# Perceiver block: token tiles normalised on POOL and gathered one by one, slot weights inside the scan loop, another order of POOL's drives

## What is computed

```python
x = x + cross_attention(ctx_1024, layernorm(x))      # 16 heads, keys and values from 1024 + 64 rows
x = x + mamba(layernorm(x))                          # see below
x = x + experts(layernorm(x))                        # see below

# mamba: xz = norm(x) @ W_in; conv of 4 taps, silu; dt = softplus(..); 16 states n per channel:
h[n] = exp(dt * A[n]) * h[n] + dt * B[n] * x         # a scan over the 64 tokens of a sequence
y    = sum_n h[n] * C[n] + x * D
out  = (y * silu(z)) @ W_out + residual

# experts: 8 experts, each with a list of 512 tokens (top_idx), W1 256x1024, W2 1024x256
gathered = x[top_idx.T]
out_e = gelu(gathered @ W1 + b1) @ W2 + b2
out[token] += out_e * combine_weight[token, e]
```

## Time and profile before

| | |
|---|---|
| time, median of 3 runs | 818.61 us (818.13 to 819.67) |
| the profiled execution | 817.9 us, of which the span from first to last instruction is 816.2 |
| busy in the span | PE 742.0 us (91%), DVE 513.0, POOL 417.0, ACT 415.3 |
| mean granted TensorE clock | 0.964 of 2.4 GHz |
| chain that ended last, by engine | PE 55%, POOL 15%, DVE 14%, issue 9%, ACT 4%, DMA 2% |
| attention and its fillers | up to about 650 us |
| last tile of the mamba layer | about 650 to 721.6 us |
| norm and gather | 721.6 to 738.1 us |
| experts and output | 738.1 to 816.2 us |

### The profile page before, as it was taken

The page is one execution under the profiler, slowest core; times in us unless marked ns, Lnnn a source line. Parts: engine busy times, 40 slices in busy tenths (PEclk is TensorE's granted clock), DMA queues, the critical chain, the costliest instruction groups (busy, mean ns, idle before and its releaser), DMA issues.

```text
span 816.2 us, 14312 instructions
## 1 busy us (share of the span) xinstructions
PE 742.0 (91%) x5387; PEld 677.1 (83%) x5387; DVE 513.0 (63%) x1104; ACT 415.3 (51%) x1118; POOL 417.0 (51%) x375
## 2 busy tenths in 40 slices
PE   4979999999999999999999999999998675889996
PEld 2569999999988999998889899888988562468885
DVE  5355556557564776888777769885798686840102
ACT  2534544554355566655566555466666264604331
POOL 3817105402620299668647986775588899500000
PEclk9999999999999999999999999999999966979998
DMA  8550020010002100300210121100111119203710
GB/s 312 216 154 2 1 65 15 1 65 15 1 1 65 41 14 14 95 14 11 67 46 9 13 72 46 12 11 1 30 20 27 23 21 343 105 0 104 259 51 29
DMA packets 48696, 48.81 MB, mean 60 GB/s; under 512 B 18340, under 2 KB 43632, under 8 KB 47472
## 3 DMA queue, kind: packets, MB, share of 16 engines
q1 hardware_dynamic: 48624, 47.85, 19.4%
HBM read 43.45 MB, written 4.26 MB: 58 GB/s over the span
## 4 chain that ended last, share of the span: by engine, by line
PE 55%; POOL 15%; DVE 14%; issue 9%; ACT 4%; DMA 2%; SPq 0%; POOLq 0%; DVEq 0%; ACTq 0%
PE psum L1587 15%; PE psum L1620 12%; PE psum L1603 4%; PE psum L1976 3%; POOL work L608 3%; PE psum L1966 3%; POOL y_sum L621 3%; POOL work L615 3%; PE psum L1560 2%; DVE work L918 2%; PE psum L1540 2%; PE psum L1642 2%; DMA wq_sb<-in_L_xattn_Wq_dram 2%; DVE rowmax L981 1%; PE psum L1670 1%
## 5 line engine op out<-in xcount | busy, mean ns | idle before, releaser
L1266 ACT ACTIVATE pt_hi<-psum 128x512 fp32r<-128x512 f32 (+1 forms) x192 | 87.3, 489 | 208.4 <-PE psum L1603 155.7
L1620 PE MATMUL psum<-kvn_hi,pt_hi 128*128 128x256 f32 x512 | 150.1, 293 | 1.0 <-DVE pt_hi L838 1.0
L1620 PE MATMUL psum<-kvn_hi,pt_lo 128*128 128x256 f32 x512 | 144.3, 282 | 0.0
L1620 PE MATMUL psum<-kvn_lo,pt_hi 128*128 128x256 f32 x512 | 144.3, 282 | 0.0
L981 DVE TENSOR_REDUCE rowmax<-psum 128x1 f32<-128x728 f32 x64 | 58.6, 915 | 82.1 <-PE psum L1587 81.9
L1620 PEld LDWEIGHTS psum<-kvn_hi,pt_hi 128*128 128x128 f32 x512 | 97.5, 190 | 1.3 <-DVE pt_hi L838 1.2
L1620 PEld LDWEIGHTS psum<-kvn_lo,pt_hi 128*128 128x128 f32 x512 | 97.7, 191 | 0.1
L1620 PEld LDWEIGHTS psum<-kvn_hi,pt_lo 128*128 128x128 f32 x512 | 97.3, 190 | 0.0
L1587 PE MATMUL psum<-kvt_hi,qk_hi 128*128 128x364 f32 (+1 forms) x384 | 90.8, 345 | 6.8 <-ACT prob L1386 4.3
L615 POOL TENSOR_TENSOR work<-work,bc 128x512 f32<-128x512 f32 x48 | 65.8, 1372 | 53.6 <-DVE work L918 53.6
L841 DVE TENSOR_TENSOR pt_lo<-psum,pt_hi 128x512 fp32r<-128x512 f32 x128 | 82.0, 682 | 8.7 <-ACT pt_hi L1266 8.7
(11 more groups left out here) (235 smaller groups left out, 1568.2 us busy)
## 6 DMA issues: line engine op xcount, KB each, us to landing
w<-in_L_ffn_W_dram SPq DMA_DIRECT2D x16, 1024.0 KB, 8.4
ctx_nat<-in_ctx_dram SPq DMA_DIRECT2D x8, 1024.0 KB, 5.2
bc<-dbc_keep SPq DMA_DIRECT2D x48, 128.0 KB, 4.7
q_keep<-q_t SPq DMA_DIRECT2D x1, 2048.0 KB, 8.4
q_cur<-q_keep SPq DMA_DIRECT2D x14, 128.0 KB, 3.1
wk_nat<-in_L_xattn_Wkv_dram SPq DMA_DIRECT2D x1, 1024.0 KB, 6.2
wq_sb<-in_L_xattn_Wq_dram SPq DMA_DIRECT2D x1, 1024.0 KB, 12.7
wv<-in_L_xattn_Wkv_dram SPq DMA_DIRECT2D x1, 1024.0 KB, 14.8
```

The costliest lines, as they stand in the source:

```text
L1266: act.activation(pt_hi[u][:, t0:t1, :], where[:, 0:(t1 - t0) * P].rearrange("p (t m) -> p t m", m=P), ACT.Copy)\
L1620: pe.matmul(PV, w[u][:, j, :], x_[slot][:, j, :], start=(j == 0 and w is pt_hi and x_ is kvn_hi), stop=False)
```

## The change

1. **POOL's order for pair 3.** Before: drives 0, 1, open, drive 2, close, drive 3, close, drive 4, close, gate, drives 5 to 15. After: drives 0, 1, open, drives 2, 3, then three times a closing followed by two drives (4 to 9), the gate, drives 10 to 15. The wait for `ld_ball` now stands ahead of the first of these closings.
2. **`w_out` of pair 2 and its addition.** PE does it after sum 13 (before: 8), DVE adds it behind scan 15 (before: 11).
3. **Slot weights.** PE computes those of two experts (eight matmuls) after each of the sums 11 to 14.
4. **Norm.** DVE takes the statistics of tiles 0 and 1 ahead of the loop, of tile 2 behind read 15, of tile 3 behind its addition. POOL, behind its last drive, does variance and power of each tile by itself, and for tiles 0 to 2 `f_nat` and `f_lo` too, with ACT's `f_hi` between them. Tile 3 stays on DVE. `f_nat` of the four tiles now lies in the two `dec` buffers.
5. **Gather.** PE adds tile by tile: group 1 of tile 0 before `w_out` of pair 3, group 1 of tiles 1 and 2 behind it, group 0 of tiles 0 to 2 once `x1` is complete, and last the eight matmuls of tile 3.

```diff
@@ gpsimd
-            drive_open(2)
-            close_unit(left[2])
-            drive_open(3)
+            for n in range(2, 4):
+                drive_open(n)
             pool.wait_ge(ld_ball, 48)
-            close_unit(left[3])
-            drive_open(4)
-            close_unit(left[4])
+            for n, u in ((4, left[2]), (6, left[3]), (8, left[4])):
+                close_unit(u)
+                drive_open(n)
+                drive_open(n + 1)
             times_gate(INLINE - 1)
-            for n in range(5, NS):
+            for n in range(10, NS):
                 drive_open(n)
-            pool.wait_ge(m_out, TT)
             link(pool.memset(fhalf[:], -0.5))
-            pool.wait_ge(f_stat, 1)
-            link(pool.tensor_scalar(fvar[:], fmv[:, :, 1], 1.0, EPS, ALU.mult, ALU.add))
-            pool.tensor_tensor(frstd[:], fvar[:], fhalf[:], ALU.pow).then_inc(f_rs, 1)
+            for t in range(TT):
+                pool.wait_ge(f_stat, t + 1)
+                link(pool.tensor_scalar(fvar[:, t:t + 1], fmv[:, t, 1:2], 1.0, EPS, ALU.mult, ALU.add))
+                link(pool.tensor_tensor(frstd[:, t:t + 1], fvar[:, t:t + 1], fhalf[:, t:t + 1], ALU.pow))
+                pool.sem_inc(f_rs, 1)
+                if t < INLINE:
+                    pool.tensor_scalar(f_nat[t], x1[:, t, :], fmv[:, t, 0:1], frstd[:, t:t + 1], ALU.subtract,
+                                       ALU.mult).then_inc(f_ln, 1)
+                    pool.wait_ge(f_hi_done, t + 1)
+                    pool.tensor_tensor(f_lo[:, t, :], f_nat[t], f_hi[:, t, :].bitcast(F32), ALU.subtract)\
+                        .then_inc(f_lo_done, 1)
@@ vector
+            def out_stats(t):
+                dve.wait_ge(m_out, t + 1)
+                link(dve.bn_stats(fstat[:, t, :], x1[:, t, :]))
+                dve.bn_aggr(fmv[:, t, :], fstat[:, t, :]).then_inc(f_stat, 1)
+            out_stats(0)
+            out_stats(1)
...
-                if n == 11:
+                if n == NS - 1:
                     mixed(INLINE - 1, psum[:, WB, 0:C])
                 if n >= 1:
                     read_open(n - 1)
             read_open(NS - 1)
+            out_stats(2)
...
+            out_stats(INLINE)
+            dve.wait_ge(f_rs, TT)
+            dve.wait_ge(f_lo_done, INLINE)
+            dve.tensor_scalar(f_nat[INLINE], x1[:, INLINE, :], fmv[:, INLINE, 0:1], frstd[:, INLINE:TT],
+                              ALU.subtract, ALU.mult).then_inc(f_ln, 1)
+            dve.wait_ge(f_hi_done, TT)
+            dve.tensor_tensor(f_lo[:, INLINE, :], f_nat[INLINE], f_hi[:, INLINE, :].bitcast(F32), ALU.subtract)\
+                .then_inc(f_lo_done, 1)
@@ tensor
+            def gather(g, k, t):
+                for part in (f_hi, f_lo):
+                    last = pe.matmul(psum[:, GB[g] + k, :], part[:, t, k * P:(k + 1) * P],
+                                     pick[:, t, g * RING:(g + 1) * RING, :].rearrange("p e s -> p (e s)"),
+                                     start=(t == 0 and part is f_hi), stop=(t == TT - 1 and part is f_lo))
+                return last
+            def slot_weight(e):
+                for t in range(TT):
+                    last = pe.matmul(psum[:, 4, 2 * e:2 * e + 2], pick[:, t, e, :], coef_hl[:, t, e, :],
+                                     start=(t == 0), stop=(t == TT - 1))
+                return last
...
                 sum_states(n)
-                if n == 8:
+                if n == NS - 3:
                     pe.wait_ge(v_y, INLINE)
                     w_out(zs[(INLINE - 1) % 2], psum[:, WB, 0:C]).then_inc(v_yo, 1)
                 if n < E + 3:
                     side_job(n)
+                if NS - 5 <= n < NS - 1:
+                    if n == NS - 5:
+                        pe.wait_ge(f_hl, 1)
+                        pe.wait_ge(m_b, 2)
+                    for e in range(2 * (n - NS + 5), 2 * (n - NS + 5) + 2):
+                        last = slot_weight(e)
+                    if n == NS - 2:
+                        last.then_inc(f_cs, 1)
+            pe.wait_ge(f_b2e, CK)
+            pe.wait_ge(f_lo_done, 1)
+            for k in range(CK):
+                gather(1, k, 0)
             pe.wait_ge(v_y, INLINE + 1)
             w_out(dtx_l, psum[:, WB, C:2 * C]).then_inc(v_yo, 1)
...
+            for t in range(1, INLINE):
+                pe.wait_ge(f_lo_done, t + 1)
+                for k in range(CK):
+                    gather(1, k, t)
             pe.wait_ge(m_out, TT)
-            slot_weights(0)
+            for t in range(INLINE):
+                for k in range(CK):
+                    gather(0, k, t)
             pe.wait_ge(f_lo_done, TT)
+            for g in range(EG):
+                for k in range(CK):
+                    gather(g, k, INLINE).then_inc(f_gat, 1)
             expert_round(0)
```

More of the change, by code:

```diff
@@ L205, in perceiver_kernel @@
         w2 = [sb(mam, f"w2_{i}", [P, FT, C]) for i in range(RING)]
+        f_nat = [d[:].rearrange("p d m -> p (d m)")[:, h * C:(h + 1) * C] for d in dec for h in range(2)]
+        f_hi = sb(mam, "f_hi", [P, TT, C], F32R)
+        f_lo = sb(mam, "f_lo", [P, TT, C], F32R)
+        fstat = sb(mam, "fstat", [P, TT, 6])
+        fmv = sb(mam, "fmv", [P, TT, 2])
+        fvar = sb(mam, "fvar", [P, TT])
+        frstd = sb(mam, "frstd", [P, TT])
+        fhalf = sb(mam, "fhalf", [P, TT])
         open_ = ExitStack()
@@ L219, in perceiver_kernel @@
         o_lo = sb(mam, "o_lo", [P, C], F32R)
-        f_nat = sb(mam, "f_nat", [P, TT, C])
-        f_hi = sb(mam, "f_hi", [P, TT, C], F32R)
-        f_lo = sb(mam, "f_lo", [P, TT, C], F32R)
         res_nat = sb(mam, "res_nat", [P, TT, C])
[L224 to L228, removed]
         mam.close()
@@ L1502, in _ @@
                 act.wait_ge(f_ln, t + 1)
-                act.activation(f_hi[:, t, :], f_nat[:, t, :], ACT.Copy).then_inc(f_hi_done, 1)
+                act.activation(f_hi[:, t, :], f_nat[t], ACT.Copy).then_inc(f_hi_done, 1)
             expert_round(0)
@@ L1920, in slot_weights @@
             def slot_weights(r):
-                pe.wait_ge(f_hl, 1)
                 if not isinstance(r, int):
@@ L1925, in slot_weights @@
                 for e in range(E):
-                    for t in range(TT):
-                        last = pe.matmul(psum[:, 4, 2 * e:2 * e + 2], pick[:, t, e, :], coef_hl[:, t, e, :],
-                                         start=(t == 0), stop=(t == TT - 1))
+                    last = slot_weight(e)
                 last.then_inc(f_cs, 1)
             def expert_round(r):
[L1933 to L1942, removed]
+                if not isinstance(r, int):
+                    for g in range(EG):
+                        if g == 1:
+                            pe.wait_ge(f_turned, E * (r + 1))
+                        for k in range(CK):
+                            for t in range(TT):
+                                last = gather(g, k, t)
+                            last.then_inc(f_gat, 1)
                 pe.wait_ge(f_gate, CK * (EG * r + 1))
```

## The result

The changed kernel takes 808.6 us (median of 4 runs, 804.6 to 809.8) against 818.8 (four runs of the kernel before, 818.1 to 819.7): the ratio is 0.9866, with an interval from 0.9838 to 0.9895. Forecast were 806.0 in a range of 802.5 to 811.

What follows compares the result with a forecast made beforehand. The bound was the serial stretch from pair 3's first drive (672.8) to the first expert matmul (738.1), and TensorE's clock. Gains of 13.4 or 12.2 us, taken as 12.7 from 817.9, gave 805.2, median about 806, range 802.5 to 811.

Steps and rivals of the forecast that it cites:

- Part 1: POOL in pair 3: two drives after each closing put scan 5 at 688.5, scan 11 at 701.2; gain 4.0 us.
- What is late next is PE and ACT: Loop once drive 5 is early: low-clock sum and transposes take 2.6 us a state; ACT's decays wait behind its copy.
- Part 2: `w_out` of pair 2 after sum 13: scan 15 at 708.6 instead of 714.55, 5.9 us early in all.
- Part 3: Slot weights after sums 11 to 14: eight cost 0.85 us at high clock; removing this part would return 0.8.
- Part 4: Norm on POOL tile by tile: `f_nat` 0.7 us, tile 2 ready at 716.7, nothing waits, 2 us of cover.
- Part 5: Gather split by tile: 20 matmuls take 4.7 us, last eight 1.9; PE through at 724.5 instead of 738.1.
- The sum: First drive of pair 3 to first expert matmul (the block): gain 13.4 us at high clock, 12.2 low-stretch, 12.7 taken.
- Rival (a): Clock falls again between 700 and 724: short stretch gains 8 to 11 us, chance 0.2; long gains 4, chance 0.05.
- the forecast proper: Time of the whole changed kernel between 802.5 and 808 us, chance 0.62.
- The rule on the clock gate: Micro-idles between matmul groups swing TensorE's clock; by it a fall between 700 and 724 is forecast, 809 or so.
- Rival (c): Change does little: scans' end sets time, drive order and late projection give nothing; gain 8 to 9 us, chance 0.08.
- rival (b): PE's clock does not rise at 689.4 at all: block ends at 740 to 749, 2 to 11 us slower; chance 0.03.

Runs made afterwards that it cites:

- experiment 2: Changed kernel with POOL's old order of drives and closings: 808.6 us, ratio to the kernel before 0.9886, block 55.5 us.
- the repetition: Changed kernel run and profiled again without any edit: 807.6 us, ratio to the kernel before 0.9867, block 52.5 us, clock high at the loop's end.
- experiment 4: Changed kernel with norm and gather as in the kernel before: 815.4 us, ratio to the kernel before 0.9964, block 62.9 us.
- experiment 5: Changed kernel with pair 2's projection back after sum 8, its addition at n = 11, run twice: 804.3 us (block 59.9) and 807.5 us (block 52.0).
- experiment 6: Changed kernel with all 32 slot weight matmuls in front of sum 0: 807.9 us, block 51.6 us.
- experiment 3: Kernel before with only POOL's new order of drives and closings: 814.4 us, ratio to the kernel before 0.9942, block 61.9 us.

## Why the prediction was right, step by step

- **Part 1, drive order.** Laid out with scan 5 at 15.7 us behind the first drive; measured 14.8 and 15.4. Scan 11 was to gain 4.0 and gains 4.0 (28.2 us behind the first drive, before 32.2). Worth 2.6 at the end by the layout (experiment 2's expectation), 3.0 by experiment 2, 3.5 alone. The choice of the layout without the low stretch of the old loop was right: it is gone in every profile of the new order. What the account "What is late next is PE and ACT" leaves out is that scans 6 and 8 still wait for POOL, 2.8 us in all in the first profile and 2.1 in the repetition.
- **Part 2, projection late.** Scan 15 predicted 35.8 us behind the first drive, measured 36.4 and 36.3. The move's share in the middle (1.7 to 1.8 us) and its return behind read 13 are both there, and net it gives nothing or costs 0.5 us (experiments 4 and 5).
- **Part 3, slot weights.** 0.8 predicted, 0.9 measured (experiment 6), at the high clock. For the low one I had 1.3 to 1.45 us for eight of them; 2.3 were measured (714.88 to 717.22 in experiment 5). The row that I had, 32 in 5.51 us from 721.67, runs at the high level up to 723.3 and mixes both. The giving back behind read 13: of 5.5 us at scan 15 the repetition keeps 2.3 at `dtx_l`; I had 5.9 and 3.0. Some 3 us go in both.
- **Part 4, POOL's norm.** The size was wrong, not the step: `f_nat` takes 1.23 us where I took 0.7, from a subtraction of 64 x 256 that takes 0.73, and tile 2 is ready 45.2 us behind the first drive, not 43.9. It still had cover: PE's gather of tile 2 began at 48.4 in that profile. A row of another form did not bound one with two per-partition operands.
- **Part 5, gather split.** Predicted 20 matmuls in PE's time behind `w_out` as the late piece, then eight more: the block ends 51.7 us behind the first drive; 52.5 in the repetition. The 0.8 is already there at the end of the addition (46.6 against 45.7), and the gather itself takes what was said, 28 matmuls of 0.235.
- **The sum.** 13.4 predicted for a high clock, 65.4 - 52.5 = 12.9 measured in the repetition, 11.4 in the first profile. Rival (a), the fall of the clock, did come true there, in a shorter form than I had (3.5 us, not 6 to 10), and cost 1.5 us; the 10.2 us between the medians lie within the 8 to 11 that I gave it. I had tied it to the two-column matmuls "just before the fall" at 723.4; in that trace they run from 721.67 to 727.2, so the clock fell among them, and the low stretch given as 695.2 to 699.6 is 3.4 us of that window (its mean is 0.61). In experiment 5 it came in its long form, 7.9 us. That it is drawn anew in each execution and not bound to the slot weights, I had not seen; neither had I that the same holds for the stretch ahead of the block, where it moved the start by 2.5 us in the very profile. Of the 3.4 us between the 805.2 that I had for the profiled execution and its 808.6, the start is 2.5 and the block 1.3 (54.0 against 65.4 - 12.7), and 0.4 comes off behind it. So the median, 808.6, lies above the 802.5 to 808 of the forecast proper and in the band of rival (a), and in the profiled execution, which took 808.6 too, 2.5 us of it come from ahead of the block, which neither the forecast nor a rival had. That the number is off by only 2.6 us from 806.0 is in part luck of the draw. The fastest executions, 804.4 for the changed kernel and 816.7 for the one before on the same chip, are 12.4 us apart, close to the block's 12.9.
- **The rule on the clock gate** (the Trainium skill, TensorE: Matmul & The Clock Gate, "A second HAM failure mode: psum-queue depth-cycling"): micro-idles between groups let the clock swing. The rows agree in kind (falls at 717.9, 710.4 and 707.6 in loops of this kind), but with a high clock through the same loop in other executions of the same program. The Trainium skill, SBUF — State Buffer, "Who interferes with whom", has no contention with GpSimd for a DVE instruction with at most one SBUF input, outside the 2-port modes. POOL's `f_lo` beside DVE's scans and reads of one SBUF input (711.46, 715.09) took 0.72 to 0.73, as the subtraction of the earlier trace rows does, so the one-input case holds here.
- **Rival (c)** is out by experiments 2 and 3 for part 1 (for part 2 alone it was right: nothing gained), rival (b) did not occur.

What stays open is what sets the instant of a fall. No run here isolates it, a way to hold the clock up in the loop was not tried, and neither was an order of POOL's work that brings drives 6 and 8 earlier. Only three of the kernels were profiled twice, so most block lengths rest on one profile.

## What to carry to other kernels

Work on tiles that are final early, pulled out of a serial tail and into the waits of the engine that is idle there, gave 10.5 of the 12.9 us, about 2.3 of them because the wait had also brought a low clock; the bound then passes to the engine whose queue was filled (here PE), so each filler must be asked whether its new place is still a wait: the slot weights cost nothing before, 0.9 in the loop, some 3.3 (2.4 more than in the loop) behind the addition, and nothing in the hole ahead of sum 0. When a move is made for an engine in the middle of a loop, follow its queue to the loop's end, where a late projection gave back all that it had gained. And take the gain of a change of this size from the length of its own block in several profiles, since the draw of the clock elsewhere moves the whole time by some 5 us.

## What the runs showed of the hardware

- The granted clock differs between executions of one program: 0.87 or 1.00 in the first 20 us, 0.56 or 1.00 over 4 us at the loop's end. It moved the block from 52.5 to 54.0, and from 52.0 to 59.9.
- At the low level a sum with eight two-column matmuls takes 3.4 us from start to start, about twice the 1.77 of the high one.
- On POOL a `tensor_scalar` of 128 x 256 with two per-partition operands takes 1.23 us, and a power of one column 0.57.
